# Attention of a graph layer on one core: weights and values as high and low f32r parts, exclusion on GpSimd, first transpositions inside the next tile's scores

## The chip, the cores and the metric

One core of a Trainium2 chip runs the kernel. The metric is device time in microseconds of one execution; the profiled execution was taken apart from the timed ones. Engines are named as the profile names them: PE is TensorE, PEld its weight loads, DVE is VectorE, ACT is ScalarE, POOL is GpSimd, SP is SyncE (here it only issues DMAs).

## The reference

3125 nodes of 256 features, 100,000 weighted edges sorted by target. A graph-attention layer, a feed-forward block and a top-1 mixture of 32 experts, with layer norms between. Cut to the part that matters:

```python
q = linear(x, wq, bq); k = linear(x, wk, bk); v = linear(x, wv, bv)
scores = jnp.sum(q[dst] * k[src], axis=-1) * scale + (edge_weight[:, None] @ we + be)[:, 0]
seg_max = jax.ops.segment_max(scores, dst, num_segments=n)
exp_s = jnp.exp(scores - seg_max[dst])
denom = jax.ops.segment_sum(exp_s, dst, num_segments=n)
attn = exp_s / jnp.maximum(denom[dst], 1e-12)
out = jax.ops.segment_sum(v[src] * attn[:, None], dst, num_segments=n)
x = layer_norm(x + out + linear(x, ws, bs), g1, b1)
```

## The kernel before, in words

The edges are turned into a dense matrix. `adj` in HBM holds, for each target node, 3200 columns (25 tiles of 128, of which 125 are nodes), each the sum of the exponentials of the edge terms between that pair, and 0 where there is no edge. Attention is then dense: for a tile of 125 targets, scores against all 3200 columns, the exponential, times the row of `adj`, times the values.

The stages in time: norms and the projections q, k, v and skip, with the edge tables made beside them (to about 139 us of the profile); 512 groups that build `adj` (the "sums", to about 748 us); attention, 25 tiles; the feed-forward block and the router; the experts.

In the attention stage each engine has its own program, and semaphores order them. For a tile `t`, with buffer `s = t % 2`:

- POOL, `fetch` (L682): copies 125 row numbers into `gidx` and issues the indirect DMA that gathers 125 rows of 12,800 bytes of `adj` into `A_sb[s]`. It waits until `weigh` has used the same buffer, two tiles before.
- DVE, `exclude` (L1176): writes to `Z[s]` -1e30 where `A_sb` is 0 and 0 elsewhere, one instruction over 3200 columns.
- PE, `front` (L1503): 7 blocks of scores (six of 512 columns, one of 128), each 6 matmuls of f32r parts (q high and low, k high and low), in 4 banks. Block b waits until `guard` has emptied the bank of block b-4.
- DVE, `guard` (L1182): per block, adds the scores to `Z` and keeps the maximum; then `nmax`.
- ACT, `exps` (L840): 7 exponentials over `Z`, in place, placed between the copies of the tile before (`weights`, L852).
- DVE, `weigh` (L1196): `Z` times `A_sb` with the row sum, one instruction over 3200 columns, once all seven exponentials are done.
- PE, `back` (L1519): in 7 groups (six of 4 chunks of 125 columns, one of 1), transposes `Z` into bank 4 or 5, from which ACT copies it to `PT`; `weigh(g)` multiplies a chunk of `PT` with a chunk of `V` (f32, 256 columns), 25 chunks into one bank.
- DVE, `back` (L1201): divides by the row sum, adds the skip part, which has lain in `x1` since the projections, then the biases `bv` and `bs`, and takes the statistics of the norm.

PE runs `front(t+1)`, `back(t)`, `front(t+2)`, `back(t+1)` and so on (`skewed`, L357). DVE runs per step `guard(t)`, `back(t-2)`, `query_rest`, `weigh(t)`, `exclude(t+1)` (`pipeline`, L379). SP loads the query tile of each t back from HBM (`load_q`, L533).

In the sums stage POOL makes one-hot columns for 12 of each 16 groups (`pool_one_hots`, L654; the groups 3 and 7 of each 8 are left to DVE, `OWN`).

Of the kernel before, what the change touches and what calls it, by code (L numbers as in the profile page):

```python
# [4 lines left out]
F32 = mybir.dt.float32  # L5
# [82 lines left out]
def gnn_moe(nc, x, src, dst, edge_weight, wq, bq, wk, bk, wv, bv, ws, bs, we, be, g1, b1, g2, b2,  # L88
            w_ff1, b_ff1, w_ff2, b_ff2, router_w, router_b, W1, eb1, W2, eb2, out):
    ctx = ExitStack()  # L90
    with ctx:
# [19 lines left out]
        q_dram = nc.dram_tensor("q_dram", [NT, P, KH * TILE], F32)  # L111
# [41 lines left out]
        V_buf = sb("V", [P, NT * D])  # L153
        V = V_buf[0:TILE, :].rearrange("p (t d) -> p t d", d=D)

        x1 = sb("x1", [TILE, NT, D])
        ARENA = 19050
        arena = sb("arena", [P, ARENA])
# [35 lines left out]
        hT, qs = (view(2 * KH * TILE).rearrange("p (s k t) -> p s k t", s=2, k=KH) for _ in range(2))  # L194
# [9 lines left out]
        stage = view(RING * GROUP * LO).rearrange("p (s k l) -> p s k l", s=RING, k=GROUP)  # L204
        assert at[0] <= SBLK * SUB * TABW
# [5 lines left out]
        at[0] = 0  # L211
        PT = view(2 * NT * TILE).rearrange("p (s j d) -> p s j d", s=2, j=NT)
        Z = view(2 * ROW).rearrange("p (s c) -> p s c", s=2)
        A_sb = view(2 * ROW).rearrange("p (s c) -> p s c", s=2)
        assert at[0] - 2 * ROW >= step_end
# [18 lines left out]
        k_flat = kT[:, :, :, :].rearrange("p k j l -> p (k j l)")  # L234
        lg, work, hot32, total, upto, fresh = (k_flat[:, i * RT:(i + 1) * RT] for i in range(6))
# [53 lines left out]
        mx, mxr, nmax, den, rden = (small(n) for n in (8, 1, 2, 2, 2))  # L289
        has = small(2)  # L290
# [18 lines left out]
        gath_in = [sem(f"gath_in{b}") for b in range(SBLK)]  # L309
# [28 lines left out]
        xs_in, w_in, out_done = ([sem(f"{n}{q}") for q in range(ES)] for n in ("xs_in", "w_in", "out_done"))  # L338

        NWB = NW // TILE  # L340
        NCONST = 10
# [5 lines left out]
        q_v = q_dram.ap().rearrange("t p c -> p t c")  # L347
        edge_tab_v = edge_tab.ap().rearrange("(p k) c -> p k c", k=PC)
# [5 lines left out]
        KV_FIRST = 7  # L354
        SPREAD_AT, ROWS_AT, COUNTS_AT = 4, 10, 11

# [124 lines left out]
        def _(sp):  # L481
# [30 lines left out]
            for b in range(SBLK):  # L512
                sp.wait_ge(gath_in[b], 16 * SUB)
# [41 lines left out]


# [1100 lines left out]
```

## Time and profile before

| | us |
|---|---|
| timed runs, median of 3 | 1658.9 (1656.93 to 1661.5) |
| profiled execution | 1657.33 |
| its span | 1655.6 |
| PE busy | 1505.8 (91%) |
| DVE busy | 1068.7 (65%) |
| ACT busy | 920.7 (56%) |
| POOL busy | 724.4 (44%) |

The span is what the profile covers; the profiled execution's own time is 1.7 us more. PE is the busiest engine; a busy PE in this profile is not PE at its peak, since the ends of matmuls are modelled. What counts for a stream of matmuls is the distance from start to start. TensorE's granted clock is given as a share of 2.4 GHz.

### The profile page before, as it was taken

What the parts mean: (1) busy time and instruction counts of PE and PEld (TensorE: products, weight loads), DVE (VectorE), ACT (ScalarE), POOL (GpSimd) and SP (SyncE); (2) the same over time, 40 slices, a digit from 0 to 9 for tenths busy, and PEclk for the clock granted to TensorE, in tenths of its full rate; (3) what the DMA queues carried; (4) which work ended last, traced back from release to release, by engine and by line L of the source; (5) the groups of instructions that cost most, each with busy time, mean ns of one, the idle gap of its engine ahead of it and who ended that gap; (6) DMA issues with size and microseconds to landing.
All of it is one profiled execution on the core that took longest, in us unless ns stands there. A gap on an engine that the chain in (4) does not pass through costs nothing.

```text
span 1655.6 us, 40803 instructions
## 1 busy us (share of the span) xinstructions
PE 1505.8 (91%) x9862; PEld 1311.8 (79%) x9862; DVE 1068.7 (65%) x2995; ACT 920.7 (56%) x2928; POOL 724.4 (44%) x1149
## 2 busy tenths in 40 slices
PE   5979999999999999995999999999999979974777
PEld 5968888988988988894888888888888869962444
DVE  7725888888888888885355544555455557985222
ACT  4748999999999999992333333333333334530111
POOL 0046777777777777771011101111011006752554
PEclk9989999999999999997999999999999989986988
DMA  8263444444444444446221122211221130124663
GB/s 190 41 181 78 111 108 112 110 109 113 108 111 110 108 112 109 110 112 154 84 77 67 67 82 84 72 66 71 84 83 67 53 77 28 61 69 117 189 184 99
DMA packets 220684, 164.30 MB, mean 99 GB/s; under 512 B 45888, under 2 KB 212749, under 8 KB 217412
## 3 DMA queue, kind: packets, MB, share of 16 engines
q1 hardware_dynamic: 189690, 96.79, 23.8%
q0 software_dynamic: 16544, 57.40, 10.0%
q10 hardware_dynamic: 14400, 9.55, 2.0%
q8 instruction: 19, 0.31, 0.1%
q14 instruction: 31, 0.25, 0.0%
HBM read 82.33 MB, written 85.50 MB: 101 GB/s over the span
## 4 chain that ended last, share of the span: by engine, by line
PE 65%; DVE 14%; issue 9%; DMA 4%; another core or an unknown queue 2%; ACT 2%; DVEq 2%; POOL 1%; ACTq 0%; POOLq 0%; SPq 0%
PE bank L1527 17%; PE bank L1494 13%; PE bank L1515 13%; DVE arena L1157 7%; DVE arena L1130 4%; PE bank L1534 4%; PE bank L1478 3%; PE bank L1559 3%; PE bank L1415 3%; PE bank L1567 3%; DMA arena<-rows_dram,arena 2%; DMA arena<-adj,gidx 1%; PE bank L1420 1%; PE bank L1422 1%
## 5 line engine op out<-in xcount | busy, mean ns | idle before, releaser
L833 ACT ACTIVATE arena<-bank,tables 128x128 f32<-128x128 f32 x2048 | 562.2, 375 | 43.6 <-PE bank L1478 42.9
L1494 PEld LDWEIGHTS bank<-arena 128*125 128x125 f32 x4096 | 536.4, 188 | 61.6 <-ACT arena L833 39.6
L1494 PE MATMUL bank<-arena 128*125 128x128 f32 x4096 | 559.3, 275 | 21.5 <-DVE arena L1130 9.6
L667 POOL TENSOR_SCALAR arena<-iota_row,held 128x125 f32<-128x125 f32 x768 | 464.8, 619 | 132.3 <-PE bank L1494 129.3
L1157 DVE SCALAR_TENSOR_TENSOR arena<-arena,tables,bank 125x128 f32<-125x128 f32 x1023 | 350.4, 342 | 93.9 <-DVE arena L1157 90.3
L859 ACT COPY arena<-bank 125x500 f32<-125x500 f32 (+1 forms) x175 | 90.7, 532 | 381.0 <-PE bank L1534 381.0
L1527 PE MATMUL bank<-V,arena 125*125 125x256 f32 x1250 | 296.4, 382 | 5.6 <-ACT arena L859 5.6
L1130 DVE TENSOR_TENSOR arena<-iota_row,tables 128x250 f32<-128x250 f32 x640 | 267.2, 418 | 9.0 <-issue 8.8
L1527 PEld LDWEIGHTS bank<-V,arena 125*125 125x125 f32 x1250 | 223.4, 188 | 38.0 <-ACT arena L859 10.3
L687 POOL COPY gidx<-arow 125x1 uint32 (+1 forms) x25 | 37.4, 1496 | 463.3 <-DVE wk_sb L1198 463.3
L1198 DVE CUSTOM_DVE_ANT_0 arena<-arena 125x3200 f32<-125x3200 f32 x25 | 87.3, 3494 | 222.5 <-ACT arena L842 222.5
L1478 PE MATMUL bank<-dist_rhs,arena 128*128 128x512 bf16 x512 | 193.7, 379 | 0.9 <-issue 0.9
L1515 PE MATMUL bank<-k_hi,q_hi 128*125 128x512 f32 (+1 forms) x350 | 139.6, 399 | 18.5 <-DVE wk_sb L1188 14.2
L1515 PE MATMUL bank<-k_lo,q_hi 128*125 128x512 f32 (+1 forms) x350 | 134.7, 385 | 0.0
L1515 PE MATMUL bank<-k_hi,q_lo 128*125 128x512 f32 (+1 forms) x350 | 134.6, 384 | 0.0
L842 ACT ACTIVATE arena<-arena,wk_sb 125x512 f32<-125x512 f32 (+1 forms) x175 | 115.8, 679 | 20.0 <-DVE wk_sb L1193 20.0
L1188 DVE CUSTOM_DVE_ANT_0 arena<-bank,arena 125x512 f32<-125x512 f32 (+1 forms) x175 | 103.0, 632 | 32.0 <-PE bank L1515 22.2
L942 ACT ACTIVATE arena<-bank,V 64x64 f32<-64x64 f32 x80 | 20.3, 302 | 141.7 <-issue 62.7
L1515 PEld LDWEIGHTS bank<-k_hi,q_hi 128*125 128x125 f32 x350 | 66.9, 191 | 39.9 <-DVE wk_sb L1188 21.4
L1534 PE MATMUL bank<-ident,arena 125*125 125x125 f32 x625 | 94.5, 276 | 2.7 <-issue 2.7
L1534 PEld LDWEIGHTS bank<-ident,arena 125*125 125x125 f32 x625 | 88.7, 190 | 9.4 <-issue 3.1
L1515 PEld LDWEIGHTS bank<-k_hi,q_lo 128*125 128x125 f32 x350 | 66.7, 190 | 14.5
(240 smaller groups left out, 1588.0 us busy)
## 6 DMA issues: line engine op xcount, KB each, us to landing
adj<-arena SPq DMA_DIRECT2D x256, 224.0 KB
adj<-arena SPq DMA_DIRECT2D x256, 26.0 KB
q_dram<-arena ACTq DMA_DIRECT2D x25, 125.0 KB
wq_sb<-q_dram SPq DMA_DIRECT2D x25, 125.0 KB, 7.9
rows_dram<-tables SPq DMA_DIRECT2D x25, 125.0 KB
rows_dram<-x SPq DMA_DIRECT2D x25, 125.0 KB
arena<-term_rows SPq DMA_DIRECT2D x192, 8.0 KB
V<-in_x SPq DMA_DIRECT2D x5, 560.0 KB
```

The costliest lines, as they stand in the source:

```text
L667: ins = nc.gpsimd.tensor_scalar(Xs[:, j % STAGES, k, :], iota_row[:, 0:TILE], held[:, h, c:c + 1], None, ALU.is_equal)
L833: ins = nc.scalar.activation(Ys[:, q, k, :], dist_bank(j)[:, k * LO:(k + 1) * LO], ACT.Relu, scale=nval_tab[:, bass.ds(i, 1)])
L842: ins = nc.scalar.activation(Z[0:TILE, s, c:c + n], Z[0:TILE, s, c:c + n], ACT.Exp, bias=nmax[:, s:s + 1])
L859: nc.scalar.copy(PT[0:TILE, s, j:j + n, :], bank[4 + g % 2][0:TILE, 0:n * TILE].rearrange("p (n d) -> p n d", n=n)).then_inc(pt_ready, 1)
L1130: ins = V_.tensor_tensor(Xs[:, s, cols, :], iota_row[:, 0:TILE].unsqueeze(1).to_broadcast([P, SUB, TILE]), code_tab[:, bass.ds(g * GC + k ...
L1157: ins = V_.scalar_tensor_tensor(stage[0:TILE, r, k, :], prev, keep_tab[0:TILE, bass.ds(g * GROUP + k, 1)], ps, ALU.mult, ALU.add)
L1188: V_.tensor_tensor_reduce(out=Z[0:TILE, s, c:c + n], in0=bank[b % 4][0:TILE, 0:n], in1=Z[0:TILE, s, c:c + n], scale=1.0, scalar=-BIG, op0= ...
L1478: mm(dist_bank(j)[:, 0:GC * LO], dist_rows[:, j // LOADG, c:c + CHUNK], dist_rhs[:, :], start=True, stop=True).then_inc(dist_done, 1)
L1494: ins = mm(o, Xs[:, j % STAGES, k, :], Ys[:, j % STAGES, k, :], start=(k % SUB == 0), stop=(k % SUB == SUB - 1))
L1515: ins = mm(bank[b % 4][0:TILE, 0:n], q[:, s, k, :], v[:, k, j, :].rearrange("p j l -> p (j l)"), start=(i == 0), stop=(i == len(parts) - 1))
L1527: ins = mm(bank[6 + s][0:TILE, 0:D], PT[0:TILE, s, j, :], V[:, j, :], start=(j == 0), stop=(j == NT - 1))
L1534: ins = tr(bank[4 + g % 2][0:TILE, j * TILE:(j + 1) * TILE], Z[0:TILE, s, (j0 + j) * LO:(j0 + j) * LO + TILE], ident[0:TILE, 0:TILE])
```

## The change

- In `back` on PE, a chunk of attention weights times a chunk of values is no longer one f32 matmul of 256 columns but two f32r matmuls: the high part of the weights with low and high part of the values side by side (512 columns, one whole bank), and the low part of the weights with the high part of the values (256 columns). ACT's copy out of the transposition bank now writes the high part (`p_hi`); a new DVE instruction per group, `weight_rest`, writes the low part (`p_lo`) from the bank and `p_hi`. `p_hi` and `p_lo` have two slots of one group each.
- The value parts are made by POOL in the sums stage, three instructions of 125x256 a tile (bias `bv` added, high part copied, low part subtracted), behind the groups 3, 7 and 11 of a turn of 16.
- `exclude` moves from DVE to POOL in two pieces (2048 and 1152 columns). POOL's order per tile is: first piece, `fetch` of the next tile, second piece, skip bias. The first piece waits for the gathered rows and for the fourth group of transpositions two tiles before.
- `weigh` on DVE is split into the 7 blocks, each released by its own exponential, and stands between the `weight_rest` of the tile before; the row sum is reduced from 7 parts.
- The first two groups of transpositions of tile t stand in `front(t+1)`, behind blocks 4 and 5, and so do their `weight_rest` in `guard(t+1)`.
- The skip part goes to HBM beside the query tile, comes back per tile (`load_skip` on SP), gets `bs` on POOL (`skip_bias`), and DVE's `back` reads it. The results of the first 23 tiles go to HBM (`store_y`) and come back behind the last scores. `x1` now lies where the keys lay.

```diff
-        x1 = sb("x1", [TILE, NT, D])
+        v_parts = sb("v_parts", [P, 2, NT * D], F32R)
+        x1 = kT[:, :, :, :].rearrange("p k j l -> p (k j l)")[0:TILE, :].rearrange("p (t d) -> p t d", d=D)
...
+        Y_PARTS = ((0, 5), (5, 14), (14, NT - 2))
+        EARLY_TR = (4, 5)
...                                                     # SP
-            with sp.Fori(2, NT // 2) as i:
-                load_q(2 * i, 0, i)
-                load_q(2 * i + 1, 1, i)
-            load_q(NT - 1, 0, NT // 2)
+            load_q(4, 0, 2)
+            for t in range(NT - 2):
+                load_skip(t + 2)
+                store_y(t)
+                if t + 5 < NT:
+                    load_q(t + 5, (t + 5) % 2, (t + 5) // 2)
 
             sp.wait_ge(s_ready, len(SCH) * NT)
+            for i, (t0, t1) in enumerate(Y_PARTS):
+                for s in range(2):
+                    sp.wait_ge(y_stored[s], 16 * ((t1 + 1 - s) // 2))
+                for rows_ in (slice(0, EVEN), slice(EVEN, TILE)):
+                    sp.dma_start(x1[rows_, t0:t1, :], y_v[rows_, t0:t1, :]).then_inc(y_got[i], 16)
...                                                     # POOL
+            def value_parts(step, t):
+                v = node_tile(V, t)
+                hi, lo = (v_parts[0:TILE, w, bass.ds(t * D, D)] for w in (1, 0))
+                if step == 0:
+                    nc.gpsimd.tensor_tensor(v, v, row["bv"][0:TILE, :], ALU.add).then_inc(v_split, 1)
+                elif step == 1:
+                    nc.gpsimd.tensor_copy(hi, v).then_inc(v_split, 1)
+                else:
+                    nc.gpsimd.tensor_tensor(lo, v, hi.bitcast(F32), ALU.subtract).then_inc(v_split, 1)
+            V_AT = (3, 7, 11)
...
-            each(pool, fetch)
+            E_CUT = 4 * 4 * LO
+            def exclude(t, s, u, part):
+                c = slice(0, E_CUT) if part == 0 else slice(E_CUT, ROW)
+                if part == 0:
+                    pool.wait_ge(a_in[s], 16 * (u + 1))
+                if not (isinstance(t, int) and t < 2):
+                    pool.wait_ge(tr_ready, len(TRG) * (t - 2) + 4 if part == 0 else len(TRG) * (t - 1))
+                pool.sem_inc(pool_mark, 1)
+                nc.gpsimd.tensor_scalar(Z[0:TILE, s, c], A_sb[0:TILE, s, c], 0.0, -BIG, ALU.is_equal, ALU.mult).then_inc(excluded, 1)
+            def gather_step(t, s, u):
+                exclude(t, s, u, 0)
+                if not (isinstance(t, int) and t + 1 >= NT):
+                    fetch(t + 1, 1 - s, u + s)
+                exclude(t, s, u, 1)
+                skip_bias(t - 1, 1 - s, u + s - 1)
...                                                     # ACT
-                    nc.scalar.copy(PT[0:TILE, s, j:j + n, :], bank[4 + g % 2][0:TILE, 0:n * TILE].rearrange(
+                    nc.scalar.copy(p_hi[0:TILE, (s + g) % 2, 0:n, :], bank[4 + g % 2][0:TILE, 0:n * TILE].rearrange(
...                                                     # DVE
+            def weight_rest(t, s, g):
+                j, n = TRG[g]
+                dve.wait_ge(pt_ready, len(TRG) * t + g + 1)
+                slot = (s + g) % 2
+                V_.tensor_tensor(p_lo[0:TILE, slot, 0:n, :], bank[4 + g % 2][0:TILE, 0:n * TILE].rearrange(
+                    "p (n d) -> p n d", n=n), p_hi[0:TILE, slot, 0:n, :].bitcast(F32), ALU.subtract).then_inc(p_split, 1)
 
             def guard(t, s, u):
-                dve.wait_ge(excluded, t + 1)
                 for b, (c, n) in enumerate(SCH):
+                    if b in (0, 4):
+                        dve.wait_ge(excluded, 2 * t + (2 if b else 1))
...
+                    if b in EARLY_TR and not (isinstance(t, int) and t == 0):
+                        weight_rest(t - 1, 1 - s, EARLY_TR.index(b))
...
+            def mix(t, s, u):
+                last = isinstance(t, int) and t + 1 >= NT
+                for g in range(0 if last else len(EARLY_TR), len(TRG)):
+                    weight_rest(t, s, g)
+                    if not last:
+                        weigh(t + 1, 1 - s, g - len(EARLY_TR))
+                    if g == len(EARLY_TR) and not (isinstance(t, int) and t + 2 >= NT):
+                        query_rest(t + 2, s, u + 1)
+                if not last:
+                    for b in range(len(SCH) - len(EARLY_TR), len(SCH)):
+                        weigh(t + 1, 1 - s, b)
...
-            pipeline(dve, (guard, 1), (back, 3), (early_statistics, 2), (later_query_rest, 0), (weigh, 1), (exclude, 0))
+            pipeline(dve, (guard, 1), (first_weigh, 1), (mix, 2), (back, 2), (early_statistics, 2))
...                                                     # PE
+            def transpose_weights(t, s, g):
+                j0, n = TRG[g]
+                pe.wait_ge(p_ready, len(SCH) * t + g + 1)
+                wait_from(pe, p_split, len(TRG) * t + (g - 1 if g >= 2 else 0))
...
             def back(t, s, u):
...
                     for j in range(j0, j0 + n):
-                        ins = mm(bank[6 + s][0:TILE, 0:D], PT[0:TILE, s, j, :], V[:, j, :], start=(j == 0), stop=(j == NT - 1))
+                        c = slice(j * D, (j + 1) * D)
+                        whole = (bank[6 + s][0:TILE, 0:2 * D], p_hi[0:TILE, slot, j - j0, :], v_parts[0:TILE, :, c])
+                        rest = (bank[6 + s][0:TILE, D:2 * D], p_lo[0:TILE, slot, j - j0, :], v_parts[0:TILE, 1, c])
+                        for o, w, v in ((whole, rest) if j == 0 else (rest, whole)):
+                            ins = mm(o, w, v, start=(j == 0 and o is whole[0]), stop=(j == NT - 1 and o is whole[0]))
                     return ins
...
+                for g in range(len(EARLY_TR), len(TRG)):
+                    weigh(g - 2)
+                    transpose_weights(t, s, g)
+                weigh(len(TRG) - 2)
                 weigh(len(TRG) - 1).then_inc(attn_done, 1)
```

## Rows read from the trace of the kernel before

**Rows 1.** The page, busy time of PE and POOL: us, share, instructions.

```profile
PE 1505.8 (91%) x9862; PEld 1311.8 (79%) x9862; DVE 1068.7 (65%) x2995; ACT 920.7 (56%) x2928; POOL 724.4 (44%) x1149
```

**Rows 2.** The chain of waits, attention stage: start us, length us, what.

```profile
828.08 8.96 PE bank L1515 x42
...
1290.99 8.96 PE bank L1515 x42
```

**Rows 3.** 21 tiles: PE, PEld, DVE, ACT, POOL busy (instructions), PEclk, DMA share, GB/s.

```profile
828.08:1314.07 485.99, 481.01 (x2458) 408.08 (x2458) 259.08 (x568) 166.17 (x314) 59.30 (x42) 1.00 0.20 74
```

**Rows 4.** Timeline, PE: start us, length us, engine, line, operation, operands.

```profile
903.26 0.39 PE L1515 MATMUL bank<-k_lo,q_hi 128*125 128x512 f32 x1
903.49 0.39 PE L1515 MATMUL bank<-k_hi,q_lo 128*125 128x512 f32 x1
...
906.09 0.27 PE L1515 MATMUL bank<-k_hi,q_hi 128*125 128x128 f32 x1
906.19 0.27 PE L1515 MATMUL bank<-k_lo,q_hi 128*125 128x128 f32 x1
...
911.72 0.60 PE L1534 MATMUL bank<-ident,arena 125*125 125x125 f32 x4
912.15 1.89 PE L1527 MATMUL bank<-V,arena 125*125 125x256 f32 x8
...
913.88 0.60 PE L1534 MATMUL bank<-ident,arena 125*125 125x125 f32 x4
```

**Rows 5.** Groups of instructions by line and form, 1000 to 1300 us.

```profile
L1188 DVE CUSTOM_DVE_ANT_0 arena<-bank,arena 125x512 f32<-125x512 f32 x78 | 50.8, 689 | 14.4 <-PE bank L1515 9.0 <-DVE arena L1180 4.4
L1198 DVE CUSTOM_DVE_ANT_0 arena<-arena 125x3200 f32<-125x3200 f32 x13 | 45.4, 3494 | 115.5 <-ACT arena L842 115.5
L1180 DVE TENSOR_SCALAR arena<-arena 125x3200 f32<-125x3200 f32 x13 | 23.7, 1825 | 0.0
```

**Rows 6.** The gather's line: landing counted from its start, us.

```profile
DMA to landing us min/median/max: 15.1/15.9/19.8
```

**Rows 7.** Timeline, POOL and DVE around a gather's issue.

```profile
1293.49 1.83 DVE L1180 TENSOR_SCALAR arena<-arena 125x3200 f32<-125x3200 f32 x1
...
1293.74 1.62 POOL L687 COPY gidx<-arow 125x1 uint32 x1 [19.44 <-DVE wk_sb L1198]
...
1296.28 1.21 POOL L690 DMA_INDIRECT arena<-adj,gidx  x1 [0.93 <-POOL gidx L687]
```

**Rows 8.** Lines of POOL: instruction, count, ns min/median/max, forms.

```profile
L687 POOL COPY gidx<-arow x25: 182/1606/1617, 743.0 to 1293.7; 125x1 uint32 x22, 125x1 uint32<-125x1 uint32 x3
...
L650 POOL COPY held<-tables x64: 205/240/410, 135.1 to 727.8; 128x32 f32 x60, 128x32 f32<-128x32 f32 x4
...
L625 POOL TENSOR_TENSOR ws_sb<-ws_sb,ident x2: 453/454/455, 15.5 to 15.9; 128x128 f32<-128x128 f32 x2
...
L701 POOL TENSOR_TENSOR x<-x,bf_row x25: 722/726/829, 1360.6 to 1460.8; 125x256 f32 x14, 125x256 f32<-125x256 f32 x11
...
L712 POOL TENSOR_SCALAR wk_sb<-wk_sb x50: 211/226/407, 1376.9 to 1478.5; 125x1 f32<-125x1 f32 x50
...
L667 POOL TENSOR_SCALAR arena<-iota_row,held x768: 590/604/868, 135.7 to 742.5; 128x125 f32<-128x125 f32 x192
```

**Rows 9.** Timeline, DVE with two inputs in SBUF beside POOL.

```profile
1398.05 0.48 DVE L1242 SCALAR_TENSOR_TENSOR x<-x,mean,g_row 125x256 f32<-125x256 f32 x1
1398.55 0.72 POOL L708 TENSOR_TENSOR tables<-tables,b_row 125x256 f32<-125x256 f32 x1
1398.61 0.94 DVE L1268 SCALAR_TENSOR_TENSOR x<-x,wk_sb,g_row 125x256 f32<-125x256 f32 x1
```

**Rows 10.** Timeline, end of the sums stage and first tile.

```profile
737.35 1.04 PE L1494 MATMUL bank<-arena 128*125 128x128 f32 x8
...
738.44 1.04 PE L1494 MATMUL bank<-arena 128*125 128x128 f32 x8
...
764.85 1.83 DVE L1180 TENSOR_SCALAR arena<-arena 125x3200 f32<-125x3200 f32 x1 [7.93 <-DMA arena<-adj,gidx]
```

More of the change, by code:

```diff
@@ L233, in gnn_moe @@
         RT = NT * NEXP
-        k_flat = kT[:, :, :, :].rearrange("p k j l -> p (k j l)")
-        lg, work, hot32, total, upto, fresh = (k_flat[:, i * RT:(i + 1) * RT] for i in range(6))
+        lg, work, hot32, total, upto, fresh = (late[:, i * RT:(i + 1) * RT] for i in range(6))
         hot = hot32.bitcast(BF16)[:, 0:RT]
@@ L289, in gnn_moe @@
         mx, mxr, nmax, den, rden = (small(n) for n in (8, 1, 2, 2, 2))
+        den_parts = small(2 * len(SCH)).rearrange("p (s c) -> p s c", s=2)
         has = small(2)
@@ L554, in _ @@
             turns(sp, put)
+            for t in range(2):
+                load_skip(t)
             for t in range(2, 4):
@@ L692, in fetch, with skip_bias @@
                     bass.IndirectOffsetOnAxis(ap=gidx[0:TILE, s:s + 1], axis=0)).then_inc(a_in[s], 16)
-            each(pool, fetch)
+            E_CUT = 4 * 4 * LO
[5 more added lines that the diff above has]
+                    pool.wait_ge(tr_ready, len(TRG) * (t - 2) + 4 if part == 0 else len(TRG) * (t - 1))
+                pool.sem_inc(pool_mark, 1)
+                nc.gpsimd.tensor_scalar(Z[0:TILE, s, c], A_sb[0:TILE, s, c], 0.0, -BIG, ALU.is_equal, ALU.mult).then_inc(excluded, 1)
+            def skip_bias(t, s, u):
+                pool.wait_ge(skip_got[s], 16 * (u + 1))
+                pool.sem_inc(pool_mark, 1)
+                nc.gpsimd.tensor_tensor(skip_in[:, s, :], skip_in[:, s, :], row["bs"][0:TILE, :], ALU.add).then_inc(skip_set, 1)
+            def gather_step(t, s, u):
[4 more added lines that the diff above has]
+                skip_bias(t - 1, 1 - s, u + s - 1)
+            fetch(0, 0, 0)
+            fetch(1, 1, 0)
+            pool.wait_ge(sums_ready, NG)
+            for part in range(2):
+                exclude(0, 0, 0, part)
+            gather_step(1, 1, 0)
+            gather_step(2, 0, 1)
+            with pool.Fori(1, NT // 2 - 1) as i:
+                gather_step(2 * i + 1, 1, i)
+                gather_step(2 * i + 2, 0, i + 1)
+            gather_step(NT - 2, 1, NT // 2 - 1)
+            gather_step(NT - 1, 0, NT // 2)
+            skip_bias(NT - 1, 0, NT // 2)
             def ffn_offset(t, s, u):
@@ L1241, in x1_scale @@
                     statistics(st1, NT - 2, NT)
+                for i, (t0, t1) in enumerate(Y_PARTS):
+                    if isinstance(t, int) and t == min(t0, 13):
+                        dve.wait_ge(y_got[i], 32)
                 V_.scalar_tensor_tensor(v, v, mean[:, bass.ds(t, 1)], row["g1"][0:TILE, :], ALU.subtract, ALU.mult).then_inc(
```

155 lines of the change are left out of this document (102 added, 53 removed).

## The prediction

> **What bounds the kernel now.** The page first: PE is busy 91% of the span, DVE 65%, ACT 56%, POOL 44% [rows 1], so the reader looks for PE's work on the path. The chain of waits then shows where the change lies: from 828.08 to 1290.99 us the 42 score matmuls of a tile come back 20 times, so a tile takes 462.9 / 20 = 23.15 us [rows 2]. The busy time of 21 tiles says who sets that pace: PE 481 of 486 us at granted clock 1.00 (2.4 GHz), DVE 259, ACT 166, POOL 59 [rows 3]. PE is the bound of this stage, and DVE works 12.3 us a tile.
>
> Start to start in the timeline [rows 4]: the f32 matmuls of attention times values take 913.88 - 912.15 = 1.73 us for 4 chunks, 0.4325 a chunk, 10.8 a tile; a group of four transpositions 912.15 - 911.72 = 0.43, so 6 x 0.43 + 0.11 = 2.7 a tile; the scores 9.0 [rows 2]. Sum 22.5; the other 0.65 us of a tile is short waits of PE, for the first copy and for the score banks.
>
> A second loop is out of sight, because nobody waits for it now: the gather. It takes 15.9 us from the start of its issue to landing [rows 6], and its issue hangs on `weigh`: DVE ends `weigh` at 1293.49, POOL's 125-number copy runs 1.62 us, the gather starts at 1296.28, 2.8 us behind [rows 7]. With two buffers that loop has had two tiles, 46 us.
>
> **The change part by part.** *Values (PE).* A chunk becomes a 512-column and a 256-column f32r matmul. The first is 903.49 - 903.26 = 0.23 us [rows 4]. For 256 columns there is no row: 128 columns take 0.10, 512 take 0.23 [rows 4], and by columns between them 0.14, which I take. A chunk then costs 0.37, 9.25 a tile, a gain of 1.55; with 0.10 it is 2.55, with 0.23 a loss of 0.7. The 0.65 of waits goes too, since a copy now has `weigh` of another group (1.5 us) in front of it. PE alone would need 9.0 + 9.25 + 2.7 = 20.9 us, 2.2 less than now. The early transpositions only move; they take the same 2.7.
>
> *DVE.* Off: `exclude` 1.83, the long `weigh` 3.5 [rows 5], `bv` and `bs` about 0.9. On: seven smaller `weigh` and seven `weight_rest`, none of which has a row; by the 0.69 of a 512-column block of `guard` [rows 5] each seven come to 6 x 0.69 + 0.3 = 4.4, and 3.5 is the low end of the first. 12.3 - 6.2 + 8.8 + 0.6 for the row sums gives 15.5 us a tile. That is below 20.9, so it costs nothing by amount; by order it can, since PE now waits for `weight_rest` behind every transposition.
>
> *Exclusion (POOL), the decisive price.* No row shows a long tensor_scalar on POOL. The nearest ones [rows 8]: a copy 205 ns for 32 columns and 182 for one, 0.74 ns a column; tensor_tensor 453 for 128 and 722 for 256, 2.1 ns a column over 0.18; tensor_scalar with compare 590 for 125 columns, against 211 for one column of another tensor_scalar, at most 3.06 ns a column, with the cost of its pointer operand inside. The first piece (2048 columns) is thus 1.7 to 6.5 us, the second (1152) 1.0 to 3.7. I take 2.1 ns, the middle row: 4.5 and 2.6 us. The compare's row is nearest in kind but has a pointer that the new instruction has not, so it is the upper end.
>
> The Trainium skill (GPSIMD Engine Reference, Engine selection) says that one-input work runs at roughly line rate there and only two-input work is about twice as slow as on VectorE. The copy's row agrees, the compare's does not; the rule's result is the first rival.
>
> *The new loop.* POOL's order is piece one of t, copy, gather of t+1, piece two of t, bias, and then piece one of t+1, which waits for that gather. One gather per turn of this loop, not two in two: the end of piece one to the start of the next gather is 0.2 for the copy (0.182 where DVE runs nothing in its way; the 1.61 of now ends together with DVE's `exclude` at 1295.3 [rows 7, 8]) plus 0.93 plus gaps, 1.3 in all; landing 15.9 later [rows 6]; then piece one. The period cannot be less than 17.2 + piece one = 17.2 + 4.5 = 21.7 us. So the gain of PE is cut off at 21.7, and the piece's price decides: 20.9 holds up to 3.7 us, today's 23.15 is reached at 5.9.
>
> *DVE against POOL.* When DVE has two inputs in SBUF and POOL has just begun to read, DVE waits: 0.94 us against 0.48 for the same kind without POOL [rows 9]. `weigh` reads `Z` and `A_sb`, both in SBUF. Count from the end of piece one: gather at 1.3, issue until 2.5, piece two until 5.1, then four blocks of `guard` and `weight_rest` (each 0.65) before `nmax`; PE's `back` can begin at 6.5 and ends at 17.4, and the last `weigh` of the next tile ends near 18.2. The gather has landed at 17.2. So the next piece one meets the last `weigh` blocks, and one of both waits, between 0 and 1.0 us; the fetch behind waits for those `weigh`. I take 0.5, period 22.2.
>
> The Trainium skill (SBUF — State Buffer, Who interferes with whom) has this as an exclusive lock for the whole instruction, and so speaks against long POOL reads beside `weigh`. Rows 9 agree (0.46 us of wait under an instruction of 0.72).
>
> *Value parts.* 75 POOL instructions of up to 0.72 us [rows 8] in groups that POOL leaves to DVE; a group lasts 738.44 - 737.35 = 1.09 us [rows 10], so they fit. 50 of them could hold DVE's one-hots by 0.46 each: 0 to 23 us, and since PE has four groups in the ring I take 2.
>
> *Start and end.* The first piece one starts at 764.85 [rows 10] and takes 4.5 instead of 1.83, and the second piece follows; the split `weigh` gives back up to 2.8 behind the exponentials. I take +2 (0 to 5). Skip loads, stores of y and their return (2.9 MB behind the last scores, with 20 us of `back` of two tiles in front of the first use) I take at nothing; if the return were late it would cost at most the 15 to 20 us by which those loads push back x.
>
> **Sum**, against the profiled execution's 1657.3 us: 22 periods at 22.2 instead of 23.15, -20.9; three tiles of start and end at PE's pace, 3 x 2.2 = -6.6; +2 and +2. 1657.3 - 23.5 = 1633.8, so 1634. The timed median is 1.6 above the profiled execution, which is inside its own spread.
>
> **Rivals.**
> 1. *POOL is cheap, PE stays the bound.* At the copy's 0.74 ns piece one is 1.7 us and the loop 18.9, under PE's 20.9. 25 x 2.2 = -55, +4: 1606; with the 256-column matmul at 0.10 us, 1581. For it: the copy's row. Against it: every compare and every two-input row of POOL.
> 2. *POOL is the bound and slower than PE was.* One mechanism: the serial loop of gather and piece one on POOL. At 3.06 ns piece one is 6.5, the loop 23.7, with a meeting of `weigh` 24.7: 22 x 0.55 = +12 or 22 x 1.55 = +34; -6.6, +4 and 2 more at the start: 1669 to 1691, middle 1680. It decides from 5.9 us of piece one, or 4.9 if each tile loses the whole 1.0 to `weigh`. For it: the compare's row; against it: its pointer.
> 3. *Nothing moves*: the gain on PE is given back tile by tile in waits for `weight_rest` or POOL, 1652 to 1662.
>
> **How the numbers follow.** My case 0.42 (1615 to 1650 by the bounds of `weigh` and the 256-column matmul), rival 1 0.25, rival 2 0.27, rival 3 0.06. A difference under 0.3% (5 us) can't be told from no change in this kernel. Faster: nearly all of the first two less a small part of mine that ends near 1652, 0.61; same 0.08; slower 0.31. The range 1596 to 1690 cuts off the low tail of rival 1 and the top of rival 2.
>
> **What would show it.** Right: in the attention stage PE busy well under 99%, its gaps at score block 4, released by DVE's `guard`, which waits for POOL; POOL's first piece starting when the gather lands, every tile; a period of first piece plus 17 us. The chunk pair at 0.37 us start to start. The 125-number copy at 0.2 us. Some `weigh` blocks near POOL's start stretched from 0.7 to several us. Wrong: first pieces under 3.7 us with PE at 99% (rival 1); a first piece over 5.9 us (rival 2); gaps of PE in `back`, in front of the value matmuls, which would be `weight_rest` coming late; a gather longer than 15.9 us because skip and y traffic shares its queues.

## The result, and the profile after

| | before | after |
|---|---|---|
| timed runs, median | 1658.43 us (1656.93 to 1661.5, 4 runs) | 1710.63 us (1707.2 to 1715.76, 4 runs) |
| profiled execution | 1657.33 us | 1710.59 us |
| its span | 1655.6 us | 1708.8 us |

The changed kernel is slower: ratio 1.0317, 95% interval 1.0295 to 1.0339. The forecast was 1634, and the time lies above its whole range. The mechanism of rival 2 took place, at a price above its upper end.

The page of the changed kernel, busy time of the engines and three groups of part 5 (busy us, mean ns of one | idle before it, and what ended it):

```profile
PE 1488.5 (87%) x9862; PEld 1290.4 (76%) x9862; DVE 1222.1 (72%) x3420; ACT 922.4 (54%) x2928; POOL 1039.9 (61%) x1300
...
L773 POOL TENSOR_SCALAR arena<-arena 125x2048 f32<-125x2048 f32 (+1 forms) x50 | 282.6, 5653 | 258.9 <-DMA arena<-adj,gidx 236.7
...
L1674 PE MATMUL bank<-v_parts,p_lo 125*125 125x256 f32 x625 | 186.0, 304 | 37.5 <-DVE p_lo L1284 37.5
...
L1307 DVE CUSTOM_DVE_ANT_0 arena<-arena 125x512 f32<-125x512 f32 (+1 forms) x175 | 195.7, 1140 | 0.8 <-ACT arena L948 0.8
```

POOL's busy time rose by 315 us, and PE is busy for a smaller share [rows 1]. L773 is the exclusion: POOL works 282.6 us on it and waits 258.9 us in front of it, 236.7 of them for the gather. On DVE the same exclusion took 1.83 us a tile [rows 5]; here its two pieces take 7.2 + 4.1 = 11.3 us. L1307 is `weigh`, whose mean for a block of 512 columns or less is 1140 ns.

By form, 800 to 1370 us, the two pieces:

```profile
L773 POOL TENSOR_SCALAR arena<-arena 125x2048 f32<-125x2048 f32 x23 | 165.8, 7208 | 238.7 <-DMA arena<-adj,gidx 218.4 <-PE bank L1640 20.3
L773 POOL TENSOR_SCALAR arena<-arena 125x1152 f32<-125x1152 f32 x23 | 94.4, 4106 | 1.7
```

(7208 - 4106) / 896 = 3.46 ns a column. The chain of waits, 748 to 1400 us, now runs through POOL and the gather and no longer through PE [rows 2]:

```profile
831.95 6.76 POOL arena L773
840.21 16.70 DMA arena<-adj,gidx
857.18 6.75 POOL arena L773
865.44 16.52 DMA arena<-adj,gidx
882.28 6.76 POOL arena L773
```

A turn is 857.18 - 831.95 = 25.2 us; the mean of 20 turns, from the fourth tile's first score matmul to the twenty-fourth's, is 25.05 against 23.15 before. Over the stretch of [rows 3]:

```profile
828.08:1314.07 485.99, 424.46 (x2262) 356.03 (x2261) 362.69 (x851) 156.93 (x294) 263.50 (x96) 0.95 0.22 79
```

PE 424 of 486 us where it had 481, at a mean granted clock of 0.95 where it had 1.00. The timeline of one tile (start us, length us, engine, line) shows how a turn passes, and a `weigh` held up inside it:

```profile
1056.39 0.39 PE L1674 MATMUL bank<-v_parts,p_hi 125*125 125x512 f32 x1
1056.62 0.28 PE L1674 MATMUL bank<-v_parts,p_lo 125*125 125x256 f32 x1
1056.73 0.39 PE L1674 MATMUL bank<-v_parts,p_hi 125*125 125x512 f32 x1
...
1057.47 7.08 POOL L773 TENSOR_SCALAR arena<-arena 125x2048 f32<-125x2048 f32 x1 [9.68 <-DMA arena<-adj,gidx]
1057.67 4.83 DVE L1307 CUSTOM_DVE_ANT_0 arena<-arena 125x512 f32<-125x512 f32 x1
...
1062.64 0.68 DVE L1307 CUSTOM_DVE_ANT_0 arena<-arena 125x512 f32<-125x512 f32 x1
1062.77 0.39 PE L1674 MATMUL bank<-v_parts,p_lo 125*125 125x256 f32 x1 [3.29 <-DVE p_lo L1284]
...
1064.62 0.18 POOL L757 COPY gidx<-arow 125x1 uint32 x1
1065.73 1.28 POOL L760 DMA_INDIRECT arena<-adj,gidx  x1 [0.94 <-POOL gidx L757]
1067.09 4.11 POOL L773 TENSOR_SCALAR arena<-arena 125x1152 f32<-125x1152 f32 x1
```

A `weigh` block that begins 0.2 us behind POOL's first piece takes 4.83 us instead of 0.68; `weight_rest` stands behind it, and PE waits 3.29 us. The chunk pair is 0.34 us here (1056.73 - 1056.39).

The last rows of after are the end of the attention stage, from its chain:

```profile
1366.03 2.88 DVE mean L1080
1368.93 0.30 DVE mean L1081
...
1374.02 0.19 DVE rstd L1094
...
1375.18 2.92 PE bank L1656 x6
```

The chain gives start and length. These are the 21 small instructions of the norm's statistics of the first 23 tiles, which the change also moved (from step `NT - 1` of the pipeline to `NT - 3`), in front of the last tile's work: 1374.21 - 1366.03 = 8.2 us in which PE has nothing, and then six score matmuls take 2.92 us where six at full clock take 1.4; the granted clock is 0.60 from 1366 to 1375 us and 0.56 in the 3.5 us behind. The first of them starts while POOL's second piece runs (to 1369.2) and takes 2.88 us instead of 0.2.

Where the 53.2 us of the spans come from, by the first score and feed-forward matmuls of both traces: sums +1.1; first to last tile's scores +44.6, of which 20 x 1.90 = 38 are the period; last tile's scores to the feed-forward +6.0; the rest +1.5.

### The profile page after: what moved, and what is told of

Its sections match the earlier page's. It is cut to its first block, busy times and chain, and to the rows that moved or that the text cites. A ratio compares the mean times of both kernels' runs of the same rounds, so it can differ in the third digit from the quotient of the medians.

```text
span 1708.8 us, 41853 instructions
## 1 busy us (share of the span) xinstructions
PE 1488.5 (87%) x9862; PEld 1290.4 (76%) x9862; DVE 1222.1 (72%) x3420; ACT 922.4 (54%) x2928; POOL 1039.9 (61%) x1300
## 4 chain that ended last, share of the span: by engine, by line
PE 39%; DMA 20%; DVE 16%; issue 12%; POOL 8%; DVEq 2%; another core or an unknown queue 1%; ACT 1%; POOLq 0%; ACTq 0%; SPq 0%
DMA arena<-adj,gidx 18%; PE bank L1626 13%; POOL arena L773 7%; DVE arena L1261 7%; DVE arena L1234 4%; PE bank L1674 3%; PE bank L1656 3%; PE bank L1610 3%; PE bank L1547 3%; PE bank L1706 3%; PE bank L1714 2%; DMA arena<-rows_dram,arena 2%; DVE arena L1307 1%; PE bank L1552 1%; PE bank L1554 1%
## 5 line engine op out<-in xcount | busy, mean ns | idle before, releaser
L773 POOL TENSOR_SCALAR arena<-arena 125x2048 f32<-125x2048 f32 (+1 forms) x50 | 282.6, 5653 | 258.9 <-DMA arena<-adj,gidx 236.7
L963 ACT CAST p_hi<-bank 125x500 fp32r<-125x500 f32 (+1 forms) x175 | 92.6, 530 | 378.6 <-PE bank L1640 378.6
L1674 PE MATMUL bank<-v_parts,p_hi 125*125 125x512 f32 x625 | 233.0, 403 | 12.3 <-DVE p_lo L1284 12.3
L1674 PE MATMUL bank<-v_parts,p_lo 125*125 125x256 f32 x625 | 186.0, 304 | 37.5 <-DVE p_lo L1284 37.5
L1307 DVE CUSTOM_DVE_ANT_0 arena<-arena 125x512 f32<-125x512 f32 (+1 forms) x175 | 195.7, 1140 | 0.8 <-ACT arena L948 0.8
L1656 PE MATMUL bank<-k_hi,q_hi 128*125 128x512 f32 (+1 forms) x350 | 146.5, 419 | 52.6 <-DVE wk_sb L1294 48.4
L1294 DVE CUSTOM_DVE_ANT_0 arena<-bank,arena 125x512 f32<-125x512 f32 (+1 forms) x175 | 106.9, 631 | 99.7 <-POOL arena L773 49.8
L1284 DVE TENSOR_TENSOR p_lo<-bank,p_hi 125x500 fp32r<-125x500 f32 (+1 forms) x175 | 108.6, 621 | 73.7 <-ACT p_hi L963 73.0
L1674 PEld LDWEIGHTS bank<-v_parts,p_lo 125*125 125x125 f32 x625 | 118.5, 190 | 47.2 <-DVE p_lo L1284 45.9
L1674 PEld LDWEIGHTS bank<-v_parts,p_hi 125*125 125x125 f32 x625 | 118.8, 190 | 33.9 <-issue 10.7
L1656 PE MATMUL bank<-k_lo,q_hi 128*125 128x512 f32 (+1 forms) x350 | 141.7, 405 | 0.0
L1640 PEld LDWEIGHTS bank<-ident,arena 125*125 125x125 f32 x625 | 96.7, 194 | 9.8
```

What stands on the lines that cost most here:

```text
L773: nc.gpsimd.tensor_scalar(Z[0:TILE, s, c], A_sb[0:TILE, s, c], 0.0, -BIG, ALU.is_equal, ALU.mult).then_inc(excluded, 1)
L1284: V_.tensor_tensor(p_lo[0:TILE, slot, 0:n, :], bank[4 + g % 2][0:TILE, 0:n * TILE].rearrange("p (n d) -> p n d", n=n), p_hi[0:TILE, slot, ...
L1307: V_.tensor_tensor_reduce(out=Z[0:TILE, s, c:c + n], in0=Z[0:TILE, s, c:c + n], in1=A_sb[0:TILE, s, c:c + n], scale=1.0, scalar=0.0, op0=A ...
L1656: ins = mm(bank[b % 4][0:TILE, 0:n], q[:, s, k, :], v[:, k, j, :].rearrange("p j l -> p (j l)"), start=(i == 0), stop=(i == len(parts) - 1))
L1674: ins = mm(o, w, v, start=(j == 0 and o is whole[0]), stop=(j == NT - 1 and o is whole[0]))
```

## The experiments

Ratios are to the kernel before on the same chip; its median there was 1621 us (sets 1 and 3) or 1662 us (sets 2 and 4), so only ratios are compared between sets. "Period" is the mean distance of the first score matmuls of neighbouring tiles over 20 turns, the fourth tile's to the twenty-fourth's. A total that was expected on the first chip's scale is compared through the ratio, times 1658.4 us.

### Set 1: exclusion back on DVE, a faster gather, both, and the exclusion alone

**1. Exclusion on DVE.** The changed kernel, with one DVE instruction over 3200 columns between `mix` and `back`; POOL keeps the gather and the skip bias.

```diff
-                exclude(t, s, u, 0)
...
-                exclude(t, s, u, 1)
...
+            def dve_exclude(t, s, u):
+                dve.wait_ge(a_in[s], 16 * (u + 1))
+                wait_from(dve, tr_ready, len(TRG) * (t - 1))
+                V_.tensor_scalar(Z[0:TILE, s, :], A_sb[0:TILE, s, :], 0.0, -BIG, ALU.is_equal, ALU.mult).then_inc(excluded, 1)
```

> The changed kernel with the exclusion back on DVE, one instruction of 3200 columns between the weights of the next tile and the sums of this one; POOL only issues the gathers and adds the skip bias. Theory A (the serial loop gather, first piece, next gather on POOL sets the period of 24.9 us): the loop has two tiles per gather again, PE or DVE sets the pace, period 20.5 to 21.5 us, total 1710.6 less 22 x 3.7 = about 1628 (1615 to 1640). Theory B (the cost is in the new DVE work, weight_rest and the split weigh, that PE waits for): period stays over 23 us, total over 1670.

Measured: 1572.8 us, ratio 0.9707 (0.9685 to 0.9729), period 20.81, longest `weigh` 693 ns. Everything else of the change is worth 2.9%; the move of the exclusion alone turns that into a loss of 3.2%. The period is as theory A has it; the total, 0.9707 x 1658.4 = 1610 us, is 5 us under its range. The window from 830 to 1230 us (columns as in [rows 3]):

```profile
830.00:1230.00 400.00, 398.24 (x2243) 337.75 (x2243) 316.38 (x866) 152.54 (x285) 71.21 (x60) 1.00 0.26 94
```

PE is busy all the time at clock 1.00, as before the change, but each tile takes 2.3 us less.

**2. Gather of 128 rows** (three rows more, which nobody reads; the exclusion stays on POOL).

```diff
+            nc.gpsimd.memset(gidx[:, :], 0).then_inc(pool_ord, 1)
...
-                    A_sb[0:TILE, s, :], None, adj.ap()[...],
-                    bass.IndirectOffsetOnAxis(ap=gidx[0:TILE, s:s + 1], axis=0)).then_inc(a_in[s], 16)
+                    A_sb[0:P, s, :], None, adj.ap()[...],
+                    bass.IndirectOffsetOnAxis(ap=gidx[0:P, s:s + 1], axis=0)).then_inc(a_in[s], 16)
```

> The changed kernel with a gather of 128 rows instead of 125 (three rows more, of row number 0, that nobody reads). In the trace 125 rows go through 5 DMA engines, 25 packets of 0.48 us each; 128 should go through 16, 8 packets each, and land in 6 to 8 us instead of 16.7. Theory A: the loop becomes 1.3 + 7 + 7.2 = 15.5 us and no longer binds, though the exclusion stays on POOL; what is left is DVE's weigh waiting for POOL's 11.3 us of reads a tile, period 21 to 23.5, total 1630 to 1685. Theory C (the long reads of POOL beside weigh are the cause, not the loop): period stays at 24.5 or more, total 1700 or more.

Measured: 1640.58 us, ratio 1.0110 (1.0073 to 1.0147), period 23.85. The gather lands after 8.2 us instead of 16.7, so the loop is cut, yet only 1.2 of 4.2 us come back. The total on the first scale is 1677 us, inside theory A's range, the period 0.35 us above its range. The gather's landing, counted from its start, in the changed kernel and here:

```profile
DMA to landing us min/median/max: 15.6/16.7/21.7
```
```profile
DMA to landing us min/median/max: 7.1/8.2/11.1
```

What ends the waits now, 800 to 1270 us:

```profile
L774 POOL TENSOR_SCALAR arena<-arena 125x2048 f32<-125x2048 f32 x20 | 144.2, 7212 | 126.9 <-PE bank L1641 126.9
```
```profile
L1675 PE MATMUL bank<-v_parts,p_lo 125*125 125x256 f32 x492 | 151.9, 315 | 47.0 <-DVE p_lo L1285 47.0
```

POOL waits for PE's transpositions, no longer for the gather, and PE waits 47 us for `p_lo`, which stands behind a `weigh` held up by POOL: 47 / 20 tiles = 2.4 of the 3.05 us that a tile is longer than in experiment 3. The rest shows in PE's own work: it is busy 369.34 / 410 x 23.85 = 21.5 us a tile at a mean granted clock of 0.96 here, and 398.45 / 400 x 20.80 = 20.7 at 1.00 in experiment 3.

**3. Both.**

> Both edits: exclusion on DVE and a gather of 128 rows. Theory A: with the exclusion off POOL the gather is not on the path any more, so its 9 us are worth nothing: the same as the exclusion on DVE alone, within 0.5%. Theory B: the same too, but over 1670.

Measured: 1559.99 us, ratio 0.9627 (0.9604 to 0.9649), period 20.80. The period is that of experiment 1, as expected; the time is not within 0.5% of it. The miss is the first tile, which in experiment 1 waits for its first gathers: 24.2 us from its first score matmul to the next tile's there, 12.1 here.

**4. The kernel before, with only the exclusion moved to POOL**, same two pieces and order.

> The kernel before with only the exclusion moved to POOL, in the same two pieces and the same order (first piece, fetch, second piece). Theory A: period 1.3 + 16 + 7.2 = 24.5 to 25 us as in the changed kernel, though the values are still f32: 22 x 1.6 = +35, total 1685 to 1705. Theory B (the other parts cost): near the kernel before, within 1%.

Measured: 1669.12 us, ratio 1.0297 (1.0275 to 1.0319), period 25.23. The old f32 matmuls with the exclusion on POOL are as slow as the new ones with it: PE's speed has no part in the loss. Period and total (1708 us on the first scale) lie just above theory A's ranges. Timeline of one turn:

```profile
1065.89 7.09 POOL L703 TENSOR_SCALAR arena<-arena 125x2048 f32<-125x2048 f32 x1 [10.70 <-DMA arena<-adj,gidx]
1066.30 7.42 DVE L1227 CUSTOM_DVE_ANT_0 arena<-arena 125x3200 f32<-125x3200 f32 x1 [5.58 <-ACT arena L870]
```

The held `weigh` ends at 1073.72, 0.74 us behind POOL's first piece, and the copy for the next gather waits for it until 1073.91. That 0.9 us a turn is in this loop and not in that of the changed kernel, whose gather takes longer.

### Set 2: is it POOL's reading that holds DVE up?

Experiments 5 to 7 add POOL work that nobody waits for to the kernel of experiment 1, where the first piece used to start.

```diff
+                    pool.wait_ge(tr_ready, len(TRG) * (t - 2) + 4)
...                                                     # 5
+                    for w_ in (wf1_sb, wf2_sb):
+                        f_ = w_[:, :, :].rearrange("p k n -> p (k n)")
+                        nc.gpsimd.tensor_scalar(f_, f_, 1.0, 0.0, ALU.mult, ALU.add).then_inc(v_split, 1)
...                                                     # 6: 14 times
+                        nc.gpsimd.memset(dist_rhs[0:TILE, :].bitcast(F32), 0.0).then_inc(v_split, 1)
...                                                     # 7: 14 times
+                        nc.gpsimd.tensor_copy(dist_rhs[0:TILE, :].bitcast(F32), v_parts[0:TILE, 1, 0:256].bitcast(F32)).then_inc(v_split, 1)
```

**5. Two long reads.**

> The changed kernel with the exclusion on DVE (as in the first experiment, 20.8 us a tile, 1572.8 us where the kernel before took 1621.2) and, in each of tiles 2 to 23, two extra POOL instructions that nobody waits for: multiply by 1.0 and add 0.0 in place over 1024 columns of the feed-forward weights, started where the first piece of the exclusion started in the changed kernel. Theory (a DVE instruction with two SBUF inputs stands behind a long POOL read): weigh, at most 693 ns in the first experiment, is stretched to 2 to 4 us in most tiles, and the period is 22 us or more, the time 1590 or more on that scale (a ratio to the kernel before of 0.985 or more). Rival (POOL beside DVE costs nothing, only the serial loop of gather and exclusion did): weigh stays under 0.8 us, the period 20.8, the ratio 0.970.

Measured: ratio 0.9667 (0.9643 to 0.9691), period 20.80, longest `weigh` 693 ns. The theory's numbers failed, but the probe did not test it: its instructions were short, and the 22 `weigh` blocks that began under one of them began when 0.87 to 0.89 of it had passed.

```profile
L787 POOL TENSOR_SCALAR wf_sb<-wf_sb 128x1024 f32<-128x1024 f32 x42 | 55.6, 1339 | 189.0 <-PE bank L1647 189.0
```

This row is the find of the set: 1339 / 1024 = 1.3 ns a column for multiply and add, where the comparison took 3.46. Both read and write f32 in SBUF with two constants.

**6. Writes alone.**

> The same kernel with 14 POOL memsets of 125x256 a tile (write only, nobody waits for them) at the same place. Theory: an instruction that only writes holds nothing of DVE's up; weigh at most 0.8 us, period 20.8 to 20.9, ratio 0.970. Rival (any POOL work beside DVE costs): weigh stretched by up to the length of one memset, some 0.2 to 0.5 us, and a period of 21 or more.

Measured: ratio 0.9655 (0.9633 to 0.9676), period 20.80, longest `weigh` 693 ns, under 14 memsets of 313 ns a tile. 110 of the 150 blocks of 512 columns overlap a memset and none is held.

**7. The same with a read.**

> The same kernel with 14 POOL copies of 125x256 a tile (read and write, nobody waits for them) at the same place; it differs from the memsets in the read alone. Theory: each copy can hold one DVE instruction by at most its own length, about 0.4 us, so weigh is stretched to about 1.1 us and not to several us, and the total is 20.8 to 21.2 us a tile, ratio 0.970 to 0.980: the length of one POOL instruction decides, not the sum of POOL's work. Rival (only the total of POOL's reads counts): the same loss per us of POOL work as in the two long instructions.

Measured: ratio 0.9766 (0.9744 to 0.9788), period 21.41, longest `weigh` 900 ns. It differs from experiment 6 in the read (and in the copies' length, 402 ns where nothing is in the way): +0.61 us a tile, more than the 0.4 allowed, with `weigh` stretched less than the 1.1 us expected and no block held longer than one copy.

**8. The statistics spread out** (kernel of experiment 3, three of the 21 instructions behind each `weight_rest` of the last tile).

```diff
-                if isinstance(t, int) and t == NT - 3:
-                    statistics(st1, 0, NT - 2)
...
+                    for make in late_ops[3 * g:3 * g + 3]:
+                        od(make())
```

> The third experiment's kernel (exclusion on DVE, gather of 128 rows; ratio 0.9627 to the kernel before) with the 21 small statistics instructions of the first 23 tiles not in one block in front of PE's last tile but three behind each weight_rest of that tile. Theory: the block stood on the chain with 8.5 us, so the time falls by 6 to 9 us against the third experiment, a ratio of 0.957 to 0.959. Rival (PE at half clock and the last tile's copies would have cost it anyway, or 21 instructions between the weight_rest delay PE as much): 0.962 to 0.964.

Measured: 1591.92 us, ratio 0.9565 (0.9545 to 0.9585), the fastest kernel of this study and 0.6% under experiment 3. From the last tile's scores to the feed-forward it takes 42.4 us against 49.1 in experiment 3; the last tile's first 30 score matmuls take 6.95 us, at full clock. The chain also has a group of eight value matmuls, four chunks, at 1.40 us:

```profile
1242.92 1.40 PE bank L1685 x8
...
1248.15 6.95 PE bank L1667 x30
```

### Set 3: what on POOL costs so much?

**9. The changed kernel again.**

> The changed kernel once more, beside the three others of this set on one chip. It should give the ratio it had (1.032), with a period of 25.0 us and POOL's first piece at 7.1 to 7.2 us; another ratio would mean that the comparison depends on the chip.

Measured: 1676.03 us, ratio 1.0334 (1.0313 to 1.0354), period 25.40, first piece 7.17 us. The ratio is that of the other chip within its interval.

**10 and 11. Other operations in the same instruction**, same columns, pieces and order.

```diff
-... A_sb[0:TILE, s, c], 0.0, -BIG, ALU.is_equal, ALU.mult)
+... A_sb[0:TILE, s, c], 0.0, 0.0, ALU.mult, ALU.add)        # 10
+... A_sb[0:TILE, s, c], 0.0, 0.0, ALU.is_equal, ALU.add)    # 11
```

> The changed kernel, in which the exclusion on POOL reads and writes the same columns in the same two pieces at the same place, but multiplies by 0.0 and adds 0.0 where it compared with 0.0 and multiplied by -1e30: it leaves the exclusion out (no pair is excluded from the maximum). Theory (the comparison is what costs on POOL; multiply and add took 1.3 ns a column in the fifth experiment): first piece 2.7 us and not 7.1, the loop 17.2 + 2.7 = 19.9 us, under PE's 20.8; period 20.8 to 21.5, ratio 0.970 to 0.985. Rival (a long instruction on POOL costs 3.5 ns a column whatever it computes, and the probe's price was that of another place): 7.1 us, period 25, ratio 1.03.

> The same with compare with 0.0 kept and the multiplication by -1e30 replaced by an addition of 0.0 (so the pairs without an edge get 1 and are not excluded from the maximum). Theory (the comparison alone sets the price): first piece 7.1 us, period 25, ratio 1.03. Rival (what costs is the multiplication by -1e30, or the pair of operations): first piece 2.7 to 5 us and a ratio under 1.0.

Measured: experiment 10 1565.37 us, ratio 0.9659 (0.9629 to 0.9690), period 20.75; experiment 11 1676.26 us, ratio 1.0341 (1.0304 to 1.0378), period 25.07. The rows of both, 800 to 1270 us, 10 first:

```profile
L773 POOL TENSOR_SCALAR arena<-arena 125x2048 f32<-125x2048 f32 x22 | 45.6, 2071 | 298.3 <-DMA arena<-adj,gidx 260.2 <-PE bank L1640 38.2
...
L773 POOL TENSOR_SCALAR arena<-arena 125x1152 f32<-125x1152 f32 x22 | 26.1, 1187 | 0.7
```
```profile
L773 POOL TENSOR_SCALAR arena<-arena 125x2048 f32<-125x2048 f32 x19 | 138.2, 7272 | 199.5 <-DMA arena<-adj,gidx 158.3 <-PE bank L1640 41.2
```

Multiply and add take (2071 - 1187) / 896 = 0.99 ns a column, POOL's own waits for DVE included (the shortest first piece is 1.89 us); the comparison takes 3.5 with either second operation. Experiments 10 and 11 differ in the first operation alone, so the price is the comparison's. The ratio of experiment 10 lies a little under the range expected, since the piece is shorter than the 2.7 us taken. With 2.07 us for it the loop is 25.05 - 7.2 + 2.07 = 19.9 us, under PE's tile of 20.8, and nothing of the loss is left, although `weigh` blocks still stretch to 2.4 us: in this run such blocks are inside DVE's reserve.

**12. Six short reads a tile** (experiment 5 with six instructions).

> The kernel of the first experiment (exclusion on DVE, 20.8 us a tile, ratio 0.970) with six POOL instructions a tile that nobody waits for, multiply by 1.0 and add 0.0 in place over 1024 columns of the feed-forward weights; the fifth experiment had two, and no weigh began in the first part of one. Theory (a DVE instruction with two SBUF inputs that begins while a POOL instruction reads waits for the reading part, about 0.6 of the instruction): weigh blocks of 0.68 stretched to at most 0.68 + 0.75 = 1.45 us, three or four a tile; period 21.3 to 22.5, ratio 0.98 to 0.995. Rival (POOL beside DVE costs nothing by itself): weigh stays at 0.69 us, ratio 0.970.

Measured: ratio 1.0021 (1.0002 to 1.0039), period 23.56, longest `weigh` 1.56 us. POOL work for which nobody waits costs 2.75 us a tile, more than the upper end of what was expected. Four of the seven blocks of a tile wait, 0.88 + 0.24 + 0.64 + 0.84 = 2.6 us over their own 0.68 (columns as in the timeline above):

```profile
1064.19 1.04 POOL L789 TENSOR_SCALAR wf_sb<-wf_sb 128x1024 f32<-128x1024 f32 x1 [0.19 <-POOL wf_sb L789]
1064.21 1.56 DVE L1316 CUSTOM_DVE_ANT_0 arena<-arena 125x512 f32<-125x512 f32 x1
...
1066.30 0.92 DVE L1316 CUSTOM_DVE_ANT_0 arena<-arena 125x512 f32<-125x512 f32 x1
...
1066.87 1.26 POOL L789 TENSOR_SCALAR wf_sb<-wf_sb 128x1024 f32<-128x1024 f32 x1 [0.19 <-POOL wf_sb L789]
1067.35 1.32 DVE L1316 CUSTOM_DVE_ANT_0 arena<-arena 125x512 f32<-125x512 f32 x1
...
1068.61 1.52 DVE L1316 CUSTOM_DVE_ANT_0 arena<-arena 125x512 f32<-125x512 f32 x1
```

So the block is real, and it costs by how often it happens on a DVE that PE waits for. The theory's share of 0.6 is wrong here: each of the four is let go 0.14 us before its POOL instruction ends (for the first 1064.21 + 1.56 - 0.68 = 1065.09 against 1065.23). The sum of POOL's reads does not set the price: these six, 7.3 us a tile, cost 2.75 us, the 14 copies of experiment 7, 8.5 us a tile, cost 0.61.

### Set 4: could the exclusion have stayed on POOL?

**13. Multiply and minimum** (`1e30, 64.0, ALU.mult, ALU.min` in the line of experiment 10).

> The changed kernel with the exclusion on POOL computed as multiply by 1e30 and minimum with 64: a pair without an edge gets 0 and one with an edge 64, so pairs without an edge stand 64 below in the maximum, and their weight is 0 as before. Theory (the comparison alone is dear): first piece about 2.0 us, period 20.8, ratio 0.966. Rival (every operation but multiply and add is): first piece about 7 us, period 25, ratio 1.03.

Measured: ratio 1.0333 (1.0306 to 1.0360), period 25.06, first piece 7.3 us. The rival's numbers hold: this pair is as dear as the comparison. Whether that is the minimum or the multiplication by 1e30 was not separated; multiplications by 0.0 and 1.0 were cheap.

**14. The same with the gather of 128 rows and the statistics spread.**

> The same with the gather of 128 rows and the statistics spread as in the eighth experiment (exclusion on POOL by multiply and minimum). If the first is at 0.966: the first tile's wait for the gather goes (8 us) and the block of statistics (8 us), so a ratio of 0.955 to 0.958, no better than the eighth experiment's 0.9565, since PE sets the pace of 20.8 us in both. If the exclusion on POOL still costs DVE something on the path: above 0.960.

Measured: ratio 1.0051 (1.0033 to 1.0069), period 23.92, about 5% above experiment 8, which differs in the exclusion's engine and operation alone. With loop and statistics mended, the dear instruction on POOL still costs 23.92 - 20.80 = 3.1 us a tile, and as in experiment 2 PE waits for `p_lo`, 44.6 us in 800 to 1270 us.

## Why the prediction was wrong, point by point

- **What bounds the kernel** was read rightly. PE was the bound, and the hidden loop became it. Of the signs named for the forecast, the gaps of PE at the score blocks came (48.4 us released by `guard`, whose DVE waits 49.8 us for POOL), but so did three that were named against it: a first piece over 5.9 us, waits for `p_lo` in `back` (37.5 + 12.3 us), and a gather longer than 15.9 us.
- **Values on PE**: a chunk pair was put at 0.37 us; a group of 8 matmuls takes 1.40 (experiment 8), so 0.35. PE's tile was put at 20.9 and measured at 20.8 (experiments 1, 3, 8).
- **DVE**: put at 15.5 us a tile. In experiment 1 it is 316.38 / 400 x 20.8 = 16.5 with the exclusion's 1.82 in it, so 14.6 without. That it could cost by order and not by amount was right: PE waits for `p_lo`.
- **The step that failed is the price of the exclusion on POOL.** The prediction took 2.1 ns a column, the tensor_tensor's row, gave the compare's row as upper end (3.06 ns), and argued it down by its pointer operand. It measured 3.46, the first piece 7.2 us against 4.5 taken and 6.5 allowed. The compare's row was the right one; the price per column was above it because that row, 590 ns for 125 columns [rows 8], was reduced by a fixed cost of 211 ns that is 7208 - 3.46 x 2048 = 122 ns in fact; with it, 590 ns would have given 3.7. Experiments 10 and 11 show it is the operation that costs: multiply and add 0.99 ns, comparison 3.5; multiply by 1e30 and minimum (experiment 13) are as dear as the comparison.
- **The new loop** was right in form: 17.2 + 7.1 = 24.3, measured 25.05. Most of the other 0.8 us is the gather, median 16.7 us where it was 15.9 [rows 6]; the sum also left out the 0.3 us from landing to the first piece (840.21 + 16.70 = 856.91 against 857.18). In experiment 4, without the skip and y transfers, the gather lands after 15.6; but in experiment 7, which has these transfers, the median is 15.9, so why it is longer stays open.
- **DVE against POOL** was also mis-sized: it was put at 0 to 1.0 us because the row at hand had a POOL instruction of 0.72 [rows 9]. Under one of 7.1 us a block waits up to 4.3 us. In the changed kernel this hides partly in the loop, since both run at once; with the loop cut the exclusion on POOL still costs 3.1 us a tile (experiments 2 and 14), and in experiment 2 waits for `p_lo` are 2.4 of them.
- **Copy of the 125 numbers**: 0.2 forecast, 0.18 measured.
- **Value parts in the sums stage**: 2 us forecast, +1.1 measured.
- **Start**: 2 us forecast; the first tile takes 29.1 us against 22.6, as the first piece is 7.12 us at 767.26 and the second follows.
- **End**: forecast as part of a gain of 6.6 us, three tiles of start and end at PE's pace. From the last tile's scores to the feed-forward it took 6.0 us more instead. The move of the statistics in front of the last tile stood in the changed code and was not priced: it cost 8.2 us of chain, and experiment 8 gets 0.6% of the time back by spreading them.
- **The sum**: period 25.05 instead of 22.2, 22 times, is 63 of the 77 us between forecast and profiled execution; start and end and the smaller terms are the other 14.
- **The rivals**: rival 1's number for multiply and add is what experiment 10 shows (period 20.75); its rule of line rate does not hold for a comparison. Rival 2 had the mechanism and, at 6.5 us, a first piece that was still too short, so even its top, 1691, was passed. The Trainium skill (GPSIMD Engine Reference, Engine selection) says that one-input work is roughly line-rate on GpSimd: the traces fit it for multiply and add, 0.99 ns a column; the comparison and the pair with the minimum take 3.5 times as much.

The Trainium skill (SBUF — State Buffer, Who interferes with whom) says that a DVE instruction with two SBUF inputs contends with GpSimd instructions that read and not with those that only write. Experiments 6 and 7 agree (693 ns against 900). The prediction named the lock for the whole instruction and still priced a meeting at 0 to 1.0 us, beside a first piece that it put at 4.5 us itself: the length of the POOL instruction is the order of one meeting's price. In these traces it is an upper bound and not the price, and [rows 9] had already shown that: DVE began at 1398.61 under an instruction that ran to 1398.55 + 0.72 = 1399.27, so a lock to its end would be a wait of 0.66 us, and 0.46 was measured. The prediction read this row as agreement. In that section of the Trainium skill the words on the whole instruction stand with DVE's two-port modes; for two inputs in SBUF it gives no length.

## What to carry to other kernels

Price a moved instruction by a row of the same operation on the new engine, not by the middle of other operations; where the nearest in kind is the dearest, believe it. Moving work to an idle engine puts it into that engine's order: write down the loop that arises (here copy, gather, first piece) and the point from which it decides, and leave room for the price being wrong. On POOL, the length of one reading instruction matters beside the sum, since DVE's two-input instructions wait behind it (0.61 us a tile for 14 copies of 0.4 to 0.6 us, 2.75 for six reads of 1.2 us). Count the partitions of a gather too: three rows more halved its time.

## What was not expected of the hardware

- On POOL, tensor_scalar over 2048 columns takes 2.07 us with multiply and add and 7.2 us with a comparison, or with multiply by 1e30 and minimum.
- DVE is let go before a long comparison ends. In the changed kernel the held `weigh` ends 5.03 us behind POOL's start, less its own 0.68: 4.35 of 7.08 us. In experiment 4 it ends 7.83 behind, less its own 3.49: 4.34. With multiply and add it is let go 0.14 us before the end (1064.21 + 1.56 - 0.68 against 1065.23). The 4.35 us are 61% of the comparison's first piece, but not a fixed share: the statistics' first instruction, 0.2 us by itself, begins under the second piece, which runs from 1365.10 to 1369.20, and ends at 1368.91, so it is let go after 3.6 of 4.1 us, 88%. Why the comparison lets DVE go where it does stays open.
- A gather of 125 rows of 12,800 bytes lands after 16.7 us, one of 128 rows after 8.2. While it runs, the first keeps 31.8% of the 16 DMA engines busy, about 5 of 16 (experiment 1, 900 to 908 us; the columns are packets, MB, share):

```profile
q0 software_dynamic: 85, 1.09, 31.8%
```

The Trainium skill (DMA: Bandwidth & Descriptors, Why a DMA increments its semaphore by 16 and not by 1) says that a DMA is spread over the largest number of engines up to 16 that divides the outer size on both sides. For 125 that is 5 and for 128 it is 16; the row and the landing times agree.
